# Mixture-of-experts stage of a two-layer kernel: the weight blocks become the stationary operand and the token rows the moving one

## The chip, the cores and the metric

The kernel runs on 1 core of one Trainium2 chip. The metric is the device time of one launch in microseconds. Three runs of the kernel before gave 438.8, 442.28 and 443.53 us; their median is 442.28 us. Matrix products run on TensorE (PE in the profile), with a sequencer of its own that reads its instructions in order (PEldq in the rows); VectorE is DVE, ScalarE is ACT, GpSimd is POOL, SyncE is SP.

## The reference

The input is x, 4 batches of 256 tokens of 128 values. Two layers of cross attention follow, each with a feed-forward part; the last of these is a mixture of 8 experts. All parts add to x. What the change touches is the last one:

```python
t = x.reshape(-1, D)                      # 1024 tokens, D = 128, normalised
probs = jax.nn.softmax(t @ Wg, axis=-1)   # 8 experts
top_v, top_i = jax.lax.top_k(probs, 2)    # two experts for each token
comb = ...                                # their shares, zero elsewhere
for e in range(E):
    h = jax.nn.silu(t @ W1[e]) * (t @ W3[e])      # 512 inner values
    out = out + comb[:, e:e + 1] * (h @ W2[e])    # back to 128
```

## The kernel before

**Attention and the first feed-forward part** fill the first three quarters of the time. Eight passes (two layers of four batches) compute scores, exponentials and the product with the values, head by head, and the other steps of the neighbouring batches are put between the heads.

**The experts.** The 1024 tokens are handled in two halves of 512. Each token has two experts, so a half has 1024 rows. They are sorted by expert into up to 15 slots of 128 rows (`SLOTS`), every slot with a single expert, so there are 30 slots, k = 0 to 29. Which expert a slot has is known only at run time: `expert_id` holds the numbers, and TensorE's sequencer loads the number of slot k with `value_load` (L798) and computes from it the addresses of that expert's weights (`bass.ds(chosen[k], 1)`). A computed address is an instruction of its own on that sequencer (FUSED_REGOPS in the rows). All weights and token rows are kept as two f16 parts, a high and a low one (index s), and a product of two such numbers is made of three matmuls: high by high, high by low, low by high.

A slot goes through three steps:

- `gu` (gate and up, `gate_up`, L811): the 128 token rows, transposed in `takenT`, are the stationary operand and 512 columns of W1[e], then W3[e], move. Three matmuls each, six in all, into `p_misc` and `p_sc`, 128 rows by 512. ACT makes the silu of the first (`gated`, L1327) and DVE multiplies by the second (`product`, L1151) into `hp`.
- `hT` (`hidden_t`, L822): four transposes of 128 by 128 on TensorE turn the product into `p_o`; ACT takes its high part as f16 (`high`, L1333) and DVE the low one (`low`, L1155), into one of two buffers of `hh`.
- `dn` (`down`): four matmuls with both parts of W2[e] side by side as 256 moving columns (L830) and four with the high part alone (L833). ACT copies the columns of the low part to `y_low` (L1339) and DVE adds them (`result`, L1164). The rows of the first half go out by SP (L1580), those of the second by an indirect DMA of POOL (L1438).

**The order of the work** is written down before anything is built: `schedule()` sorts all steps by places from the tables PLACES, SHIFTED and REST, and every engine issues its part of each step in that one order. In the expert stage, `gu` of slot k stands at k, `hT` at k + 1.3 and `dn` at k + 2.6. The first slots share the order with the last pass's projections (L531, L746, L754), the norm of the last tokens, and `compare`, `rank`, `count` and `place`, which sort the second half into its slots. After the last slot, `back` reads the rows from memory and `mix` adds them to x.

Of the kernel before, what the change touches and what calls it, by code (L numbers as in the profile page):

```python
# [5 lines left out]
ALU = mybir.AluOpType  # L6
# [34 lines left out]
    0: {"max": (-4.62, 1.13), "sum": 1.39, "av": (2.76, 1.36), "f_ln": 7.78, "f_xn": -8.15, "f_xT": -1.23,  # L41
        "up0": (-2.85, 0.45), "round": 7.95, "floor": 6.62, "nodes": -8.25, "slope": 5.04, "interp": 7.44,
# [3 lines left out]
        "q0": (6.87, 0.66), "v1": 0.08, "zeros": -2.67, "wipe": -0.41, "init": (2.09, 2.98), "stack": 7.76,  # L46
        "rows": 7.86},
    1: {"max": (9.13, 1.48), "av": (-1.31, 0.11), "f_ln": 12.82, "f_xn": 17.1, "f_xT": -17.07, "up0": (6.69, 1.39),
        "round": -18.46, "floor": 7.56, "nodes": -9.32, "slope": 5.47, "interp": -10.23, "ident": 10.47,
# [3 lines left out]
        "split": (6.74, 1.32), "consts": 0.86, "ex_ln": (0.38, 1.49), "ex_xn": (5.71, 1.53), "ex_xT": (9.95, 0.83),  # L53
        "logits": (1.71, 2.04), "route": 12.72, "shares": 9.48, "compare": 22.49, "rank": 18.69, "best": 28.46,
        "count": 24.36, "place": 10.34, "send": 30.88, "fetch": 3.74, "gT": (17.26, 1.85), "rows": 11.84,
        "weights": 11.47},
# [4 lines left out]
    (0, 'aT'): (4.38, 0.28), (0, 'av'): (-0.45, 0.6), (0, 'bounce'): -1.01, (0, 'down0'): -3.31,  # L61
    (0, 'f_ln'): -7.47, (0, 'f_xT'): -3.24, (0, 'f_xn'): 3.18, (0, 'floor'): 4.93, (0, 'ident'): 3.17,
# [15 lines left out]
    (2, 'interp'): 3.09, (2, 'k0'): (5.7, 0.21), (2, 'k1'): 2.14, (2, 'max'): (1.54, 1.0), (2, 'nodes'): 2.15,
    (2, 'oT'): (5.18, 1.02), (2, 'q0'): (3.7, 1.01), (2, 'q0_ln'): -5.43, (2, 'q0_xT'): -3.12, (2, 'q0_xn'): -1.13,
    (2, 'q1'): 6.18, (2, 'q1_ln'): 4.41, (2, 'q1_xT'): 5.37, (2, 'q1_xn'): 4.83, (2, 'round'): 1.89,  # L80
    (2, 'rows'): 0.74, (2, 'sT'): 3.27, (2, 'slope'): 2.61, (2, 'stack'): -3.62, (2, 'sum'): 2.0,
    (2, 'up0'): (1.55, 0.28), (2, 'v0'): (3.05, 1.03), (2, 'v1'): -0.89, (2, 'wipe'): 5.04,
# [13 lines left out]
    (4, 'max'): (2.36, 1.01), (4, 'nodes'): 4.81, (4, 'oT'): (3.9, 2.04), (4, 'oT1'): (24.7, 0.49),
    (4, 'place'): 10.66, (4, 'q1'): 13.68, (4, 'q1_ln'): 8.29, (4, 'q1_xT'): 11.57, (4, 'q1_xn'): 10.37,
    (4, 'rank'): 17.2, (4, 'round'): 3.81, (4, 'route'): 3.68, (4, 'rows'): 4.05, (4, 'sT'): 3.63,
    (4, 'send'): 20.25, (4, 'shares'): 17.27, (4, 'slope'): 6.05, (4, 'split'): (2.95, 1.2), (4, 'stack'): -0.22,
    (4, 'stage'): (0.67, 1.64), (4, 'up0'): (3.08, 0.42), (4, 'v1'): 5.5, (4, 'weights'): 21.41,  # L100
# [5 lines left out]
    (5, 'logits'): (4.57, 1.56), (5, 'max'): (2.22, 1.14), (5, 'nodes'): 4.91, (5, 'oT'): (-0.41, 1.49),
    (5, 'oT1'): (3.4, 1.43), (5, 'place'): 20.85, (5, 'q1'): 12.67, (5, 'q1_ln'): 6.8, (5, 'q1_xT'): 11.2,
    (5, 'q1_xn'): 9.96, (5, 'rank'): 10.48, (5, 'round'): 2.45, (5, 'route'): 12.73, (5, 'rows'): 1.38,
    (5, 'sT'): -5.5, (5, 'send'): 10.6, (5, 'shares'): 4.61, (5, 'slope'): 4.93, (5, 'split'): (0.78, 2.24),
# [32 lines left out]
def schedule():  # L142
# [127 lines left out]
    for k in range(2 * SLOTS):  # L270
        placed += [(k, ("gu", k)), (k + 1.3, ("hT", k)), (k + 2.6, ("dn", k))]
# [34 lines left out]
def build(nc, t, out):  # L306
    ctx = ExitStack()
    with ctx:
# [215 lines left out]
        def _(pe):  # L524
# [290 lines left out]
            def hidden_t(k):  # L815
                pe.wait_ge(hp_done, k + 1)
                if k == 0:
                    pe.wait_ge(o_free, 6 * B)
                if k >= 2:
                    pe.wait_ge(hl_done, k - 1)  # L820
# [830 lines left out]
```

## Time and profile before

| what | value |
|---|---|
| median of 3 runs | 442.28 us (438.8 to 443.53) |
| the profiled execution's own time | 441.79 us |
| its span | 440.0 us |
| mean granted TensorE clock | 0.944 of full |
| PE / PEld / DVE busy | 87% / 51% / 74% of the span |
| ACT / POOL busy | 55% / 46% of the span |
| last chain: PE / DVE / POOL | 56% / 20% / 7% of the span |

The span runs from the first to the last instruction; 1.8 us lie around it. Busy times of PE contain the time in which a matmul drains while the next one already runs, so the distance between two starts says what one costs and not its duration. Instructions of a sequencer (register work, waits) are not counted as busy. Engine names with a q behind them are sequencers.

### The profile page before, as it was taken

The page shows a single profiled execution, that of the slowest core. Times are in us where ns is not written, and L with a number is a line of the kernel's source. Part 1 is how long each engine was busy: PE and PEld are TensorE (multiplying, and loading weights), DVE is VectorE, ACT ScalarE, POOL GpSimd, SP SyncE. Part 2 cuts the span into 40 slices and gives each one's busy share as a digit, 9 for nine tenths or more (in the row PEclk, how much of TensorE's full clock was granted, in tenths as well). Part 3 has the DMA queues.
Part 4 walks back from the last instruction along what each step waited for, and adds up shares of the span by engine and source line. Part 5 has one row for each costly group of instructions (what it writes and reads, how often), then busy time and mean ns, then how long its engine had stood idle before and what let it go on. Part 6 is the DMA issues. An engine that isn't in the chain of part 4 may idle for free.

```text
span 440.0 us, 8296 instructions
## 1 busy us (share of the span) xinstructions
PE 381.7 (87%) x2779; PEld 223.3 (51%) x2779; DVE 326.9 (74%) x677; ACT 241.4 (55%) x473; POOL 201.3 (46%) x259
## 2 busy tenths in 40 slices
PE   7657799999779968997799889998799889999990
PEld 3414454575356625654544454454355465677660
DVE  5765775667776788888789899889974477676765
ACT  3713455655826471547457858766478644566551
POOL 5034898717363775357052307647141004206661
PEclk9965999999989988998899999999899999999996
DMA  7572717207301802523014203622013001411113
GB/s 188 123 193 52 161 31 165 51 1 176 77 1 37 218 0 62 131 76 117 25 55 119 79 1 109 143 73 73 6 34 103 1 13 43 123 50 49 49 49 97
DMA packets 43406, 34.70 MB, mean 79 GB/s; under 512 B 5901, under 2 KB 39757, under 8 KB 43069
## 3 DMA queue, kind: packets, MB, share of 16 engines
q1 hardware_dynamic: 42117, 31.60, 28.1%
q0 software_dynamic: 1248, 2.57, 1.8%
q8 instruction: 24, 0.39, 0.4%
q14 instruction: 17, 0.14, 0.1%
HBM read 15.13 MB, written 7.89 MB: 52 GB/s over the span
## 4 chain that ended last, share of the span: by engine, by line
PE 56%; DVE 20%; POOL 7%; issue 5%; ACT 5%; SPq 4%; DMA 3%; POOLq 0%; DVEq 0%; ACTq 0%
PE p_sc L630 8%; PE p_o L662 6%; PE p_misc L600 6%; PE p_misc L531 5%; DVE mx L909 5%; PE p_o L649 4%; SPq L1500 4%; PE p_misc L811 4%; PE p_sc L811 4%; PE p_misc L830 3%; PE p_o L822 3%; PE p_misc L704 2%; DVE xn L879 2%; DMA region<-qx 2%; POOL kS L1369 2%
## 5 line engine op out<-in xcount | busy, mean ns | idle before, releaser
L1249 ACT ACTIVATE probs<-p_sc 128x512 f32<-128x512 f32 x192 | 104.6, 597 | 73.8 <-PE p_sc L630 73.1
L909 DVE TENSOR_REDUCE mx<-p_misc 128x1 f32<-128x512 f32 x192 | 121.9, 683 | 16.2 <-PE p_misc L600 15.0
L1363 POOL TENSOR_SCALAR veps<-meanvar 128x2 f32<-128x2 f32 x16 | 3.7, 230 | 101.0 <-DVE meanvar L865 100.7
L600 PE MATMUL p_misc<-kS,qS 96*128 96x512 f16 x128 | 39.9, 387 | 5.4 <-DVE mx L909 5.3
L1405 POOL TENSOR_TENSOR psums<-probs 128x256 f32<-128x256 f32 x32 | 24.4, 763 | 39.7 <-PE p_o L656 35.8
L662 PE MATMUL p_o<-probs,v 128*32 128x256 f32 x512 | 41.6, 402 | 0.6 <-ACT probs L1249 0.6
L630 PE MATMUL p_sc<-qS,kS 128*128 128x256 f16 x256 | 41.2, 281 | 0.3
L649 PE MATMUL p_o<-probs,v 128*64 128x256 f32 x256 | 35.6, 400 | 3.4 <-ACT probs L1249 3.4
L1151 DVE TENSOR_TENSOR probs<-probs,p_sc 128x512 f32<-128x512 f32 x30 | 20.6, 685 | 22.8 <-ACT probs L1327 22.5
L630 PE MATMUL p_sc<-region 128*128 128x256 f16 x256 | 35.4, 284 | 2.2 <-DVE region L923 2.2
L1327 ACT ACTIVATE probs<-p_misc 128x512 f32<-128x512 f32 x30 | 17.9, 597 | 31.5 <-PE p_sc L811 31.5
L630 PEld LDWEIGHTS p_sc<-qS,kS 128*128 128x128 f16 x256 | 21.7, 99 | 21.4 <-issue 12.3
L630 PEld LDWEIGHTS p_sc<-region 128*128 128x128 f16 x256 | 24.7, 102 | 14.0 <-issue 5.1
L1460 POOL TENSOR_TENSOR region<-v,region 128x512 f16<-128x512 f32 x24 | 28.8, 1200 | 1.9
L1406 POOL TENSOR_TENSOR psums<-psums,probs 128x256 f32<-128x256 f32 x32 | 27.1, 845 | 2.5
L600 PE MATMUL p_misc<-region 128*128 128x512 f16 x64 | 21.1, 404 | 6.9 <-DVE cT L893 3.0
L1407 POOL TENSOR_TENSOR psums<-psums,probs 128x256 f32<-128x256 f32 x32 | 24.8, 774 | 2.5
L649 PEld LDWEIGHTS p_o<-probs,v 128*64 128x64 f32 x256 | 15.9, 138 | 18.4 <-issue 10.0
L1459 POOL CAST region<-v 128x512 f16<-128x512 f32 x24 | 15.4, 640 | 14.3 <-DMA v<-in_L_ffn_W_dram 13.4
L1155 DVE TENSOR_TENSOR probs<-p_o,probs 128x512 f16<-128x512 f32 x30 | 20.5, 684 | 1.6 <-ACT probs L1333 1.6
L879 DVE TENSOR_SCALAR xn<-x_sb,meanvar,rstd 128x128 f32<-128x128 f32 x24 | 15.0, 705 | 8.5 <-issue 5.0
L600 PEld LDWEIGHTS p_misc<-kS,qS 96*128 96x128 f16 x128 | 11.6, 100 | 17.5 <-DVE mx L909 9.4
(221 smaller groups left out, 763.7 us busy)
## 6 DMA issues: line engine op xcount, KB each, us to landing
region<-kx SPq DMA_DIRECT2D x24, 256.0 KB, 3.9
v<-in_L_ffn_W_dram SPq DMA_DIRECT2D x24, 256.0 KB, 2.7
region<-qx SPq DMA_DIRECT2D x24, 128.0 KB, 3.8
kS<-kS SPq DMA_DIRECT2D x1, 1664.0 KB
kS<-k_scratch SPq DMA_DIRECT2D x8, 192.0 KB
k_scratch<-kx SPq DMA_DIRECT2D x4, 256.0 KB, 2.8
slots_in<-qS SPq DMA_DIRECT2D x1, 975.0 KB, 10.0
slots_in<-qS SPq DMA_DIRECT2D x1, 960.0 KB, 6.0
```

The lines of the kernel that those rows point to most:

```text
L600: pe.matmul(ps, q[:, i * P:(i + 1) * P], k, start=True, stop=True).then_inc(full, 1)
L630: last = pe.matmul(p_sc[:, half, j * S:(j + 1) * S], k[:, kt * P:(kt + 1) * P], q, start=(i == 0), stop=(i == len(pairs) - 1))
L649: pe.matmul(p_o[64 * i:64 * i + 64, 0, m * S:(m + 1) * S], v0[:, b % 2, kt, h * DH0:(h + 1) * DH0], probs[:, h % 8, kt * S:(kt + 1) * S], ...
L662: last = pe.matmul(p_o[32 * j:32 * j + 32, n % 2, 0:S], v1[:, b % 2, c, h * VW:h * VW + 32], probs[:, h % 8, c * S:(c + 1) * S], start=(c ...
L811: last = pe.matmul(ps[:, k % 2, :], takenT[half][:, xs, at], w[:, bass.ds(chosen[k], 1), ws, :].rearrange("p e n -> p (e n)"), start=(i == ...
L879: last = dve.tensor_scalar(dst, x_sb[:, b * T + i, :], meanvar[:, n % 2, i, 0:1], rstd[:, n % 2, i:i + 1], ALU.subtract, ALU.mult)
L909: dve.tensor_reduce(mx[:, b % 2, i, h:h + 1], ps, AX_X, ALU.max).then_inc(free, 1)
L1249: act.activation(probs[:, h % 8, half * 512:(half + 1) * 512], p_sc[:, half, :], ACT.Exp, scale=(DH0 if layer == 0 else DH1) ** -0.5).then ...
L1405: link(pool.tensor_tensor(psums[:, h % 4, :], tiles[0], tiles[1], ALU.add))
L1406: link(pool.tensor_tensor(psums[:, h % 4, :], psums[:, h % 4, :], tiles[2], ALU.add))
L1407: pool.tensor_tensor(psums[:, h % 4, :], psums[:, h % 4, :], tiles[3], ALU.add).then_inc(sums_set, 1)
L1460: pool.tensor_tensor(low, whole, high, ALU.subtract).then_inc(stage_free, 1)
```

## The change

Slots, experts, the three-matmul products and the results stay as they are. In `gate_up` a block of 128 weight columns is now the stationary operand and the 128 token rows move, so that the output comes out with the inner values on the partitions. The transposes (`hidden_t`) go. DVE writes the product straight into `p_o`, from which ACT and DVE take the high and low parts as before, into four buffers of `hh` instead of two. `down` is written as three passes over four blocks with 128 moving columns each, all into the same 128 columns; `y_low` and DVE's addition go, and ACT's copy (`result`) writes `y_sb` itself. `dn` stands at k + 3.1 instead of k + 2.6. The numbers in PLACES, SHIFTED and REST are new throughout; the set of steps that they place is the same.

```diff
@@ schedule()
-        placed += [(k, ("gu", k)), (k + 1.3, ("hT", k)), (k + 2.6, ("dn", k))]
+        placed += [(k, ("gu", k)), (k + 1.3, ("hT", k)), (k + 3.1, ("dn", k))]
...
-    placed += [(SLOTS + 4.9 + 3.8 * i, ("mix", 0, i)) for i in range(NT)]
+    placed += [(SLOTS + 4.7 + 3.8 * i, ("mix", 0, i)) for i in range(NT)]
@@ buffers
-        hp = probs[:, 1, :].rearrange("p (a b) -> p a b", a=2)
-        hh = probs[:, 2, :].bitcast(F16).rearrange("p (b s n) -> p b s n", b=2, s=2)
-        y_low = probs[:, 3, 0:2 * P].rearrange("p (b n) -> p b n", b=2)
+        hh = probs[:, 1:3, :].rearrange("p i n -> p (i n)").bitcast(F16).rearrange("p (b s n) -> p b s n", b=4, s=2)
@@ TensorE, gate_up
-                    for i, (ws, xs) in enumerate(((0, 0), (0, 1), (1, 0))):
-                        last = pe.matmul(ps[:, k % 2, :], takenT[half][:, xs, at], w[:, bass.ds(chosen[k], 1), ws, :].rearrange("p e n -> p (e n)"),
-                                         start=(i == 0), stop=(i == 2))
+                    for f in range(FF):
+                        block = slice(f * P, (f + 1) * P)
+                        for i, (ws, xs) in enumerate(((0, 0), (0, 1), (1, 0))):
+                            last = pe.matmul(ps[:, k % 2, block], w[:, bass.ds(chosen[k], 1), ws, block].rearrange("p e n -> p (e n)"),
+                                             takenT[half][:, xs, at], start=(i == 0), stop=(i == 2))
...
-            def hidden_t(k):
...
-                for f in range(FF):
-                    last = pe.transpose(p_o[:, k % 2, f * P:(f + 1) * P], hp[:, k % 2, f * P:(f + 1) * P], ident[:, :])
-                last.then_inc(hT_full, 1)
@@ TensorE, down
-                for f in range(FF):
-                    w = ew2[:, bass.ds(chosen[k], 1), f, :, :].rearrange("p e s n -> p (e s n)")
-                    pe.matmul(ps[:, 0:2 * P], hh[:, k % 2, 0, f * P:(f + 1) * P], w, start=(f == 0), stop=False)
-                for f in range(FF):
-                    w = ew2[:, bass.ds(chosen[k], 1), f, 0, :].rearrange("p e n -> p (e n)")
-                    last = pe.matmul(ps[:, 0:P], hh[:, k % 2, 1, f * P:(f + 1) * P], w, start=False, stop=(f == FF - 1))
+                for hs, ws in ((0, 0), (0, 1), (1, 0)):
+                    for f in range(FF):
+                        w = ew2[:, bass.ds(chosen[k], 1), f, ws, :].rearrange("p e n -> p (e n)")
+                        last = pe.matmul(ps[:, 0:P], hh[:, k % 4, hs, f * P:(f + 1) * P], w,
+                                         start=(hs == ws == f == 0), stop=(hs == 1 and f == FF - 1))
@@ VectorE, product and low; result is gone
+                if k == 0:
+                    dve.wait_ge(o_free, 6 * B)
                 if k >= 2:
-                    dve.wait_ge(hT_full, k - 1)
-                dve.tensor_tensor(hp[:, k % 2, :], sg[:, k % 2, :], p_sc[:, k % 2, :], ALU.mult).then_inc(hp_done, 1)
+                    dve.wait_ge(hl_done, k - 1)
+                dve.tensor_tensor(p_o[:, k % 2, :], sg[:, k % 2, :], p_sc[:, k % 2, :], ALU.mult).then_inc(hp_done, 1)
...
@@ ScalarE, high and result
-                act.wait_ge(hT_full, k + 1)
-                if k >= 2:
-                    misc_wait(act, ("ym", k - 2))
-                act.copy(hh[:, k % 2, 0, :], p_o[:, k % 2, :]).then_inc(hh_done, 1)
+                act.wait_ge(hp_done, k + 1)
+                if k >= 4:
+                    misc_wait(act, ("ym", k - 4))
+                act.copy(hh[:, k % 4, 0, :], p_o[:, k % 2, :]).then_inc(hh_done, 1)
...
-                act.copy(y_low[:, k % 2, :], ps[:, P:2 * P]).then_inc(y_half, 1)
+                if 4 <= k < SLOTS + 4:
+                    act.wait_ge(y_kept[k % 4], 16 * (k // 4))
+                elif k >= 4:
+                    act.wait_ge(y_sent[k % 4], 16 * sent_of(k - 4))
+                ps, free = misc_wait(act, ("ym", k))
+                act.copy(y_sb[:, k % 4, :], ps[:, 0:P]).then_inc(free, 1)
```

## Rows read from the trace of the kernel before

**Rows 1.** Busy time by stretch of the span; columns as in the second line.
```profile
core 0: us, PE busy (x) PEld busy (x) DVE busy (x) ACT busy (x) POOL busy (x), PEclk, DMA share, GB/s
0.00:344.35 344.35, 301.22 (x2188) 168.27 (x2188) 263.00 (x508) 194.11 (x371) 170.13 (x226) 0.94 0.34 86
344.35:369.52 25.17, 20.86 (x146) 13.35 (x143) 17.27 (x57) 11.69 (x24) 3.04 (x5) 1.00 0.05 14
369.52:429.94 60.42, 59.58 (x449) 41.68 (x449) 41.07 (x89) 33.82 (x76) 26.62 (x28) 1.00 0.22 64
```

**Rows 2.** Timeline of TensorE in one slot: start us, us, engine, line, tiles, count.
```profile
402.17 0.82 PE L811 MATMUL p_misc<-region,probs 128*128 x3
402.83 0.81 PE L811 MATMUL p_sc<-region,probs 128*128 x3
403.48 0.60 PE L822 MATMUL p_o<-ident,probs 128*128 128x128 f32 x4
403.91 0.60 PE L830 MATMUL p_misc<-region,probs 128*128 x4
404.35 0.39 PE L833 MATMUL p_misc<-region,probs 128*128 x4
```

**Rows 3.** Instructions of lines L811, L830, L833 in the whole span, duration ns min/median/max.
```profile
L811 PEldq FUSED_REGOPS  x120: 46/46/51, 344.1 to 424.2; - x120
...
L830 PEldq FUSED_REGOPS  x120: 46/46/46, 353.9 to 429.3; - x120
...
L833 PEld LDWEIGHTS p_misc<-region,probs x120: 97/98/99, 355.6 to 429.7; 128*128 128x128 f16 x120
L833 PE MATMUL p_misc<-region,probs x120: 219/219/219, 355.7 to 429.7; 128*128 x120
```

**Rows 4.** One stretch of TensorE's sequencer, line by line, 384.98 to 386.88 us.
```profile
L830 PEldq FUSED_REGOPS  x4: 46/46/46, 385.0 to 385.4; - x4
...
L495 PEldq EVENT_SEMAPHORE  x1: 51/51/51, 385.5 to 385.5; - x1
...
L798 PEldq TENSOR_LOAD <-kx x1: 313/313/313, 385.7 to 385.7; - x1
...
L811 PEldq FUSED_REGOPS  x4: 46/46/51, 386.3 to 386.7; - x4
...
L820 PEldq EVENT_SEMAPHORE  x1: 51/51/51, 386.8 to 386.8; - x1
```

**Rows 5.** Timeline of TensorE and its weight loads in the last slot.
```profile
429.06 0.65 PE L830 MATMUL p_misc<-region,probs 128*128 x4 [0.49 <-DVE probs L1155]
429.55 0.39 PE L833 MATMUL p_misc<-region,probs 128*128 x4
...
429.05 0.47 PEld L830 LDWEIGHTS p_misc<-region,probs 128*128 128x128 f16 x4 [0.66 <-issue]
```

**Rows 6.** Timeline of TensorE: twelve 128-column matmuls at the full clock and at half.
```profile
287.96 0.84 PE L722 MATMUL p_misc<-wc,cT 96*128 96x128 f16 x12
...
206.57 1.46 PE L722 MATMUL p_misc<-wc,cT 96*128 96x128 f16 x12 [2.35 <-DVE mx L909]
```

**Rows 7.** ACT and DVE groups, 369.5 to 427.6 us: count | busy us, mean ns | idle before, releaser.
```profile
L1155 DVE TENSOR_TENSOR probs<-p_o,probs 128x512 f16<-128x512 f32 x24 | 16.4, 683 | 0.0
L1151 DVE TENSOR_TENSOR probs<-probs,p_sc 128x512 f32<-128x512 f32 x23 | 15.8, 687 | 18.4 <-ACT probs L1327 18.4
...
L1327 ACT ACTIVATE probs<-p_misc 128x512 f32<-128x512 f32 x23 | 13.7, 597 | 23.5 <-PE p_sc L811 23.5
L1333 ACT CAST probs<-p_o 128x512 f16<-128x512 f32 x23 | 13.3, 580 | 0.0
...
L1164 DVE TENSOR_TENSOR probs<-p_misc,probs 128x128 f32<-128x128 f32 x24 | 6.7, 281 | 0.0
```

**Rows 8.** Stretches on either side of a fall of the granted clock.
```profile
247.50:250.90 3.40, 1.67 (x14) 0.46 (x12) 3.30 (x5) 3.25 (x5) 0.00 (x0) 0.99 0.23 86
250.90:254.30 3.40, 3.25 (x18) 1.66 (x18) 3.33 (x8) 3.34 (x5) 0.00 (x0) 0.51 0.00 0
```

More of the change, by code:

```diff
@@ L40 @@
 PLACES = {
-    0: {"max": (-4.62, 1.13), "sum": 1.39, "av": (2.76, 1.36), "f_ln": 7.78, "f_xn": -8.15, "f_xT": -1.23,
-        "up0": (-2.85, 0.45), "round": 7.95, "floor": 6.62, "nodes": -8.25, "slope": 5.04, "interp": 7.44,
[3 rows of a table removed]
[L46 to L49, printed above, removed]
[3 rows of a table removed]
[L53 to L56, printed above, removed]
+    0: {"max": (-8.6, 1.13), "sum": 3.84, "av": (2.9, 1.22), "f_ln": 8.5, "f_xn": -7.99, "f_xT": -4.13,
+        "up0": (-3.54, 0.17), "round": 5.08, "floor": 6.91, "nodes": -8.63, "slope": 4.85, "interp": 6.1,
[3 rows of a table added]
+        "v1": -1.81, "zeros": -3.28, "wipe": -0.5, "init": (1.97, 2.97), "stack": 8.35, "rows": 7.72},
@@ new lines @@
+    1: {"max": (11.48, 1.51), "av": (2.56, 0.11), "f_ln": 8.48, "f_xn": 17.13, "f_xT": -14.69, "up0": (9.56, 1.5),
+        "round": -19.3, "floor": 1.49, "nodes": -4.8, "slope": 15.47, "interp": -7.65, "ident": 10.47,
[3 rows of a table added]
+        "split": (6.95, 0.95), "consts": 4.58, "ex_ln": (3.19, 1.49), "ex_xn": (1.82, 1.53),
+        "ex_xT": (10.28, 0.83), "logits": (2.65, 1.87), "route": 14.84, "shares": 10.12, "compare": 21.68,
+        "rank": 19.76, "best": 30.35, "count": 24.36, "place": 5.14, "send": 31.74, "fetch": 3.15,
+        "gT": (18.67, 2.21), "rows": 11.04, "weights": 10.64},
@@ L78 @@
[L78 to L82, printed above, removed]
@@ L96 @@
[L96 to L100, printed above, removed]
@@ L106 @@
[L106 to L109, printed above, removed]
-    (5, 'stack'): -8.2, (5, 'stage'): (-1.47, 2.13), (5, 'up0'): (2.12, 0.29), (5, 'v1'): 6.14,
@@ L116 @@
-    (6, 'k1'): 5.74, (6, 'logits'): (10.56, 1.25), (6, 'max'): (3.51, 1.26), (6, 'nodes'): -12.77,
-    (6, 'oT'): (9.36, 2.42), (6, 'oT1'): (5.29, 0.4), (6, 'place'): 15.05, (6, 'q1'): -4.01, (6, 'q1_ln'): 8.43,
-    (6, 'q1_xT'): 8.06, (6, 'q1_xn'): 13.98, (6, 'rank'): 13.35, (6, 'round'): -7.01, (6, 'route'): 11.83,
-    (6, 'rows'): 2.88, (6, 'sT'): -6.41, (6, 'send'): 21.24, (6, 'shares'): 13.9, (6, 'slope'): 2.81,
-    (6, 'split'): (0.76, 1.9), (6, 'stack'): -25.07, (6, 'stage'): (1.91, 2.25), (6, 'up0'): (-3.67, 0.22),
@@ L131 @@
[L131 to L139 removed]
+    (0, 'aT'): (4.27, 0.05), (0, 'av'): (-0.45, 0.6), (0, 'bounce'): 0.43, (0, 'down0'): -4.63, (0, 'f_ln'): -9.28,
@@ new lines @@
+    (2, 'round'): 1.89, (2, 'rows'): 0.7, (2, 'sT'): 3.42, (2, 'slope'): 2.67, (2, 'stack'): -2.07,
+    (2, 'sum'): 2.0, (2, 'up0'): (1.55, 0.14), (2, 'v0'): (3.05, 1.03), (2, 'v1'): -1.53, (2, 'wipe'): 3.84,
+    (2, 'y0'): (6.02, 1.79), (2, 'zeros'): 10.52, (3, 'aT'): (5.57, 1.84), (3, 'av'): (-0.45, 0.96),
+    (3, 'bounce'): 4.5, (3, 'down0'): 4.29, (3, 'f_ln'): -7.72, (3, 'f_xT'): 1.43, (3, 'f_xn'): 0.9,
+    (3, 'floor'): 1.79, (3, 'ident'): 3.84, (3, 'init'): (1.35, 1.95), (3, 'interp'): 3.55,
[3 rows of a table added]
@@ new lines @@
+    (3, 'sT'): 3.85, (3, 'slope'): 3.39, (3, 'stack'): -11.49, (3, 'sum'): 1.18, (3, 'up0'): (1.55, 0.05),
+    (3, 'v0'): (-0.24, 0.41), (3, 'v1'): 4.99, (3, 'wipe'): -0.66, (3, 'y0'): (7.01, 0.68), (3, 'zeros'): 2.49,
+    (4, 'aT'): (5.9, 2.15), (4, 'aT1'): 2.68, (4, 'av'): (-0.1, 1.02), (4, 'best'): 9.03, (4, 'bounce'): 12.73,
+    (4, 'compare'): 15.92, (4, 'consts'): 1.28, (4, 'count'): 5.69, (4, 'down0'): 7.86,
+    (4, 'ex_ln'): (11.92, 2.75), (4, 'ex_xT'): (12.88, 0.95), (4, 'ex_xn'): (0.95, 1.31), (4, 'f_ln'): 1.18,
@@ new lines @@
+    (4, 'send'): 20.04, (4, 'shares'): 17.27, (4, 'slope'): 5.84, (4, 'split'): (2.95, 1.27), (4, 'stack'): -0.22,
+    (4, 'stage'): (0.67, 1.49), (4, 'up0'): (3.08, 0.42), (4, 'v1'): 5.36, (4, 'weights'): 20.92,
+    (4, 'y0'): (6.3, 2.78), (4, 'y1'): -5.14, (5, 'aT'): (-10.57, 1.21), (5, 'aT1'): 5.06, (5, 'av'): (0.27, 1.06),
+    (5, 'best'): 19.51, (5, 'bounce'): 10.27, (5, 'compare'): 10.26, (5, 'consts'): 5.65, (5, 'count'): 12.49,
+    (5, 'down0'): 6.53, (5, 'ex_ln'): (12.17, 0.05), (5, 'ex_xT'): (10.39, 0.07), (5, 'ex_xn'): (5.32, 1.26),
@@ new lines @@
+    (5, 'sT'): -5.61, (5, 'send'): 10.6, (5, 'shares'): 4.61, (5, 'slope'): 4.93, (5, 'split'): (0.78, 2.17),
+    (5, 'stack'): -8.59, (5, 'stage'): (-1.31, 2.29), (5, 'up0'): (2.12, 0.29), (5, 'v1'): 6.14,
+    (5, 'weights'): 12.63, (5, 'y0'): (13.47, 3.01), (5, 'y1'): 16.07, (6, 'aT'): (10.66, 1.64), (6, 'aT1'): 6.96,
+    (6, 'av'): (1.47, 0.73), (6, 'best'): 18.34, (6, 'bounce'): 5.03, (6, 'compare'): 12.04, (6, 'consts'): 2.32,
+    (6, 'count'): 14.95, (6, 'down0'): -3.42, (6, 'ex_ln'): (8.32, 1.06), (6, 'ex_xT'): (10.42, 0.67),
@@ new lines @@
+    (6, 'rows'): 3.01, (6, 'sT'): -4.97, (6, 'send'): 21.28, (6, 'shares'): 16.27, (6, 'slope'): 2.03,
+    (6, 'split'): (0.76, 1.9), (6, 'stack'): -26.53, (6, 'stage'): (2.77, 2.25), (6, 'up0'): (-4.94, 0.08),
+    (6, 'v1'): 3.98, (6, 'weights'): 28.88, (6, 'y0'): (-1.33, 4.04), (6, 'y1'): 8.62, (7, 'aT'): (-17.99, 1.14),
+    (7, 'aT1'): 7.17, (7, 'av'): (0.44, 1.18), (7, 'best'): 29.98, (7, 'bounce'): 29.7, (7, 'compare'): 19.6,
+    (7, 'consts'): 12.25, (7, 'count'): 8.3, (7, 'down0'): 2.78, (7, 'ex_ln'): (10.0, 0.5),
@@ new lines @@
+    (7, 'rank'): 8.8, (7, 'round'): -7.97, (7, 'route'): 7.02, (7, 'rows'): 7.01, (7, 'sT'): -12.46,
+    (7, 'send'): 39.69, (7, 'shares'): 7.02, (7, 'slope'): 14.49, (7, 'split'): (1.23, 2.1), (7, 'stack'): 9.96,
+    (7, 'stage'): (1.82, 1.73), (7, 'up0'): (2.3, 0.64), (7, 'v1'): -4.88, (7, 'weights'): 16.47,
+    (7, 'y0'): (-4.34, 1.77), (7, 'y1'): 9.76}
+REST = [(0.0, 'oT1', 3, 0), (0.0, 'oT1', 3, 1), (1.05, 'aT1', 3), (1.67, 'h1', 3), (1.72, 'y1', 3),
+        (1.75, 'ln', 'ex', 3), (2.42, 'xn', 'ex', 3), (3.31, 'xT', 'ex', 3), (3.57, 'logits', 3),
+        (3.89, 'compare', 1), (3.92, 'rank', 1), (4.78, 'count', 1), (4.87, 'place', 1), (9.96, 'send', 1),
+        (11.23, 'fetch', 1), (14.01, 'gT', 1, 0), (15.21, 'dest'), (17.19, 'gT', 1, 1), (18.57, 'gT', 1, 2),
+        (21.71, 'gT', 1, 3), (26.1, 'route', 1), (39.62, 'shares', 1), (40.73, 'best', 1), (54.8, 'weights', 1)]
```

109 lines of the change are left out of this document (41 added, 68 removed), and 28 rows, old and new, of tables (PLACES, SHIFTED).

## The prediction

> **What bounds the kernel now.** I first cut the span at the expert stage [rows 1]. From 344.35 us, where slot 0's first matmul starts, to 369.52, where slot 7's does, TensorE is busy for 20.86 of 25.17 us: the last projections and the sorting of the second half stand between the slots. From there to its last matmul, at 429.94, it is busy for 59.58 of 60.42 us. Then 10.06 us without TensorE bring the rows back. The attention before 344.35 has none of the changed lines.
>
> Next, what a slot costs TensorE, from distances of starts [rows 2]. Six matmuls of 512 columns: 403.48 - 402.17 = 1.31 us, about 0.216 each. Four transposes: 0.43. Four matmuls of 256 columns: 0.44. Four of 128 columns: three distances in 0.39 - 0.219 [rows 2, 3], so 0.057 each, 0.22. Together 2.40 us. The stretch holds 23 `gu`, 24 `hT`, 25 `dn` and 15 other transposes: 138 x 0.216 + 96 x 0.109 + 100 x 0.109 + 100 x 0.056 + 15 x 0.109 = 58.4 of 60.4 us. So the data path bounds it. ACT and DVE are well below: 0.60 + 0.58 us and a short copy, and 0.69 + 0.68 + 0.28 us a slot [rows 7].
>
> Third, TensorE's sequencer, which busy shares leave out. L811 and L830 each have 120 address instructions, 4 for each of 30 slots [rows 3]. `gu` has four distinct weight addresses (two matrices, two parts), though six matmuls use them; the four of L833 point where L830's did, and that line shows none. So the count is one for each distinct address, and it is kept for a second use. Their recorded 46 ns is not their price. In a stretch without a wait [rows 4] four address instructions, a semaphore wait, the load of the expert's number, four more address instructions and the next wait start between 385.0 and 386.8 us. The load group takes 385.7 to 386.3, about 0.64 us; the nine others share the remaining 1.16, 0.125 to 0.13 us each. Among L830's four lie three matmuls with their loads, among L811's four lie five, and both take the same 0.4 us: to the sequencer the matmuls themselves are nearly free. The last slot shows the same on the engine [rows 5]: when TensorE has nothing queued, L830's four weight loads take 0.47 us, (0.47 - 0.098) / 3 = 0.124 us apart. A slot now asks the sequencer for 8 x 0.125 + 0.64 + 2 waits x 0.125 = 1.9 us, hidden under 2.4 us of matmuls.
>
> **The change, part by part.**
>
> Data path. `gu`: 24 matmuls of 128 columns, each with its own weight load, at 0.056 us = 1.34 us, against 1.31. Twelve such matmuls in a row took 0.84 us at the full clock, (0.84 - 0.22) / 11 = 0.056 [rows 6]. `hT` goes: -0.44. `dn`: 12 x 0.056 = 0.67, against 0.66. A slot takes 2.0 us, 0.4 less. The Trainium skill has a rule against this change (TensorE: Matmul & The Clock Gate, Back-to-back issue gap): pairs of weight load and 128-column matmul sustain only about 81 ns each. By it a slot would take an estimated 36 x 0.081 = 2.9 us. The trace does not agree: 0.056.
>
> Sequencer. `gu` now addresses four blocks of two parts of two matrices: 16 distinct addresses, not 4. `dn` addresses four blocks of two parts: 8, not 4; its third pass uses the first's again. So 24 instead of 8. One `gu` costs 16 x 0.125 + 0.64 = 2.64 us, one `dn` 8 x 0.125 + 0.125 for its wait = 1.125 us. The wait of `hT` goes. A slot costs 3.77 us of sequencer, more than the 2.0 us of matmuls and the 2.4 us of now: **the sequencer becomes the bound**. Bounds per slot: from below 2.0 us, the data path, if an address cost only its recorded 46 ns (24 x 0.046 + 0.64 + 0.125 = 1.87); from above 24 x 0.13 + 0.64 + 0.25 = 4.0. I take 3.77, as both views of the pace agree. That recorded time understates a sequencer's instruction is also in the Trainium skill (Perfetto Trace Analysis, Sequencer-only Instruction): the wait before and the push after are not recorded. By 46 ns the change would gain; by the spacing, which the trace shows, it loses.
>
> From slot 7's start to the last matmul the new order holds 23 `gu` and 26 `dn` (slots 4 to 29): 23 x 2.64 + 26 x 1.125 + 4 waits of the second half's transposes = 60.7 + 29.3 + 0.5 = 90.5 us, against 60.42: **+30.1 us**. The deep order hides the waits: `dn` stands three slots behind its `gu`, over 10 us, and its chain on ACT and DVE is four instructions of 0.58 to 0.69 us.
>
> The first seven slots, 25.17 us: their sequencer work is 7 x 2.64 + 4 x 1.125 = 23 us, but it is split by waits for ACT and DVE, behind which it cannot run ahead. If all added addresses lie bare: 7 x 12 x 0.125 + 4 x 4 x 0.125 = 12.5. If the waits cover them: 0. Up to the second projection there are gaps for it; after it two `gu` and a `dn` stand ahead of the norm's transposes and delay the sorting. I take **+3**, near the covered end, because 23 fits in 25.
>
> Removed on ACT and DVE: DVE's 0.28 us of L1164 per slot, nothing, since neither bounds; on the last slot it is bare, with a handoff: **-0.4**. ACT's copy takes over its waits for `y_sb`; behind it in ACT's queue stands the next slot's `silu`, but the store that it waits for was issued four slots earlier, 15 us, so nothing. DVE writing PSUM instead of SBUF: 0.69 us is taken as before; L1155, which reads PSUM, has 0.68. It has room to double. `high` waits for slot k - 4 instead of k - 2: nothing.
>
> The new tables. Sorting the steps by the old and the new tables, 335 of 747 change their position, most by one to five; the largest moves are the bounce of batch 1 (28 earlier) and of batch 0 (7 later) on SP's queue, POOL's weight splits (up to 5), `shares` and `route`. Their cover is the idle time of TensorE before 344.35 (43 us) and nothing says which way it goes: 0, with 3 us either way, within the 4.7 us that the runs differ by.
>
> Sum: 440.0 + 30.1 + 3 - 0.4 = 472.7 us of span, 474.5 with the 1.8 us around it. The profiled execution's own time is 0.5 below the median, so about 474 to 475.
>
> **The rivals.**
>
> *The sequencer does not bind (faster).* If two parts 128 or 512 columns apart shared a register, or an address came at its 46 ns, the data path would decide: 864 matmuls x 0.056 + 1.6 = 50.0 us against 58.4, -8.4, another -1 in the first slots, -0.4 at the end: 432 us. It decides once a slot's sequencer work is under 2.0 us. Against it: two parts did not share one [rows 3], and the live spacing [rows 5]. Left open: the moving operand had the computed address, now the stationary one has it. 0.11.
>
> *The clock falls too.* One of the falls of the granted clock to half (1.2 GHz) came after a stretch with TensorE busy for 1.67 of 3.40 us [rows 8]. Here its matmuls fill 2.0 of 3.77 us. At half clock twelve take 1.46 us [rows 6], 0.105 to 0.12 each: 36 x 0.11 = 4.0 us a slot, a little over the sequencer, and gaps no longer overlap well: 4.1 to 4.3, 23 to 25 slots, +8 to +13: 484 us. Against it: the row's busy share also counts draining, and by that count TensorE would stay near 80% busy. 0.12.
>
> *Weight loads stop overlapping*, while addresses are cheap. A load takes 98 ns [rows 3] and now has 0.056 us of columns above it; if loads ran one after another, 864 x 0.098 + 1.6 = 86.3 against 58.4, +28: 470 us, with sequencer gaps of no account. Rows 6 speak against it: twelve loads and matmuls in 0.84 us. 0.04. This is what the rule of the Trainium skill named above comes to; with its 81 ns the same sum would be 455 us, an estimate.
>
> *No change*, by a partial sharing of addresses at which sequencer and gain cancel (2.4 us a slot): 442. 0.03.
>
> **How the numbers follow.** The forecast has 0.70. Its own range is 464 (nothing in the first slots, tables -3, 3.6 us a slot) to 484 (12.5 in the first slots); the clock case reaches 489. The range 463 to 489 leaves out the first and the fourth rival and the forecast's far ends. A change of about 1% is what this kernel's runs can tell: faster 0.12, same 0.03, slower 0.85 (0.70, 0.12 and 0.04, rounded down).
>
> **What would show it.** Lines of `gu` with 480 address instructions and of `dn` with 240; their spacing 0.125 us; weight loads of TensorE idle before them by "issue"; slots 3.7 to 3.8 us apart; no change in the duration of the matmuls, ACT and DVE. It is wrong if slots come 2.0 to 2.4 us apart, or if the address count stayed near 240.

## The result, and the profile after

The changed kernel takes 476.69 us (median of 4 runs, 475.46 to 478.15); the kernel before took 441.8 (4 runs). The ratio is 1.080, with a 95% interval of 1.073 to 1.087: slower by 35 us, where the forecast had 474. The profiled execution took 477.52 us, its span is 475.7.

The first view is again the span cut at slot 0, slot 7 and the last matmul; it answers to [rows 1] (the same columns: us, busy time and count of PE, PEld, DVE, ACT, POOL, PEclk, DMA share, GB/s).

```profile
0.00:340.60 340.60, 301.00 (x2189) 167.48 (x2189) 262.71 (x508) 193.94 (x371) 169.65 (x226) 0.94 0.35 87
340.60:370.70 30.10, 25.98 (x256) 20.77 (x252) 16.22 (x52) 10.82 (x23) 3.98 (x6) 0.89 0.04 12
370.70:465.82 95.12, 86.40 (x879) 64.46 (x879) 38.89 (x66) 34.66 (x77) 25.59 (x27) 1.00 0.14 42
465.82:475.70 9.88, 0.04 (x1) 0.00 (x0) 4.87 (x21) 1.78 (x3) 1.44 (x2) 0.57 0.32 98
```

The stretch from slot 7 on grew from 60.42 to 95.12 us. PE is still busy for 91% of it, which looks like a full engine. That is the trap of this case: a matmul is recorded with 0.219 us, of which 0.056 is its share of the pace when the queue is full and some 0.16 is draining, so matmuls that start 0.06 to 0.12 us apart record as one unbroken stretch. 864 matmuls at 0.056 us and 15 transposes at 0.109 are 50 us of work, about half of the 95.

The next rows, of lines L810 (gate and up) and L820 (down) in the whole span, answer to [rows 3].

```profile
L810 PEldq FUSED_REGOPS  x480: 46/46/51, 340.4 to 459.9; - x160
...
L820 PE MATMUL p_misc<-region,probs x360: 219/227/228, 355.8 to 465.6; 128*128 x180
L820 PEldq FUSED_REGOPS  x240: 46/46/46, 355.6 to 465.3; - x120
```

There are 480 and 240 computed addresses, 16 and 8 a slot. One slot of the sequencer, 434.5 to 438.4 us, answers to [rows 4]:

```profile
L810 PEldq FUSED_REGOPS  x16: 46/46/46, 434.6 to 436.6; - x16
...
L492 PEldq EVENT_SEMAPHORE  x1: 51/51/51, 436.7 to 436.7; - x1
...
L820 PEldq FUSED_REGOPS  x8: 46/46/46, 436.8 to 437.7; - x8
...
L795 PEldq TENSOR_LOAD <-kx x1: 303/303/303, 437.8 to 437.8; - x1
L795 PEldq FUSED_REGOPS  x1: 151/151/151, 438.2 to 438.2; - x1
```

In this slot the sequencer never rests: addresses, the wait, addresses, the load of the next number, each record 0.12 us or a little more after the one before. And this is what TensorE does in that slot, the timeline that answers to [rows 2]:

```profile
434.71 1.13 PE L810 MATMUL p_misc<-probs,region 128*128 128x128 f16 x12 [0.32 <-DVE p_o L1141]
...
435.74 1.19 PE L810 MATMUL p_sc<-probs,region 128*128 128x128 f16 x12
...
436.93 1.34 PE L820 MATMUL p_misc<-region,probs 128*128 x12
...
438.59 1.12 PE L810 MATMUL p_misc<-probs,region 128*128 128x128 f16 x12 [0.32 <-DVE p_o L1141]
```

Slot 23 to slot 24 is 438.59 - 434.71 = 3.88 us, where [rows 2] had 2.40 without the second half's transposes. Twelve matmuls take 1.13 us here and took 0.84 with the queue full [rows 6]. The releaser in brackets, DVE's product, is a wrong name: that product ended at 434.39, and this step waits for the one two slots back (`hp_done` in `gate_up`). The summary of waits (engine, line, what it waited for: us in total, times, longest) says it better for the weight loads:

```profile
PEld p_misc L810 <- issue: 13.8, 29, 1.5
PEld p_misc L820 <- issue: 1.9, 7, 0.8
```

"Issue" is idle time in which the engine waited for nothing that the profile shows, that is for its own sequencer. It comes 29 times ahead of the first weight load of a slot, where the sequencer loads the expert's number.

### The profile page after: what moved, and what is told of

It is laid out like the page before. It is cut to its first block, busy times and chain, and to the rows that moved or that the text cites. A ratio compares the mean times of both kernels' runs of the same rounds, so it can differ in the third digit from the quotient of the medians.

```text
span 475.7 us, 9765 instructions
## 1 busy us (share of the span) xinstructions
PE 413.4 (87%) x3319; PEld 252.7 (53%) x3319; DVE 322.7 (68%) x647; ACT 241.2 (51%) x473; POOL 200.7 (42%) x259
## 4 chain that ended last, share of the span: by engine, by line
PE 59%; DVE 16%; ACT 8%; issue 6%; SPq 4%; DMA 3%; POOL 2%; POOLq 0%; ACTq 0%; DVEq 0%
PE p_sc L627 9%; PE p_misc L810 7%; PE p_sc L810 6%; PE p_misc L597 6%; PE p_o L659 5%; PE p_o L646 5%; PE p_misc L528 5%; DVE mx L897 4%; SPq L1483 4%; PE p_misc L820 3%; DVE p_o L1141 3%; ACT probs L1308 2%; PE p_misc L554 2%; PE p_misc L701 2%; DMA region<-qx 2%
## 5 line engine op out<-in xcount | busy, mean ns | idle before, releaser
L1141 DVE TENSOR_TENSOR p_o<-probs,p_sc 128x512 f32<-128x512 f32 x30 | 20.9, 695 | 42.8 <-ACT probs L1308 41.3
L597 PE MATMUL p_misc<-kS,qS 96*128 96x512 f16 x128 | 41.1, 394 | 5.4 <-DVE mx L897 3.8
L1388 POOL TENSOR_TENSOR psums<-probs 128x256 f32<-128x256 f32 x32 | 25.1, 783 | 39.5 <-PE p_o L653 36.6
L820 PE MATMUL p_misc<-region,probs 128*128 x360 | 39.9, 224 | 1.0 <-DVE probs L1145 0.6
L820 PEld LDWEIGHTS p_misc<-region,probs 128*128 128x128 f16 x360 | 28.4, 96 | 11.3 <-issue 1.9
L1389 POOL TENSOR_TENSOR psums<-psums,probs 128x256 f32<-128x256 f32 x32 | 26.4, 826 | 2.5
L1390 POOL TENSOR_TENSOR psums<-psums,probs 128x256 f32<-128x256 f32 x32 | 24.4, 763 | 2.5
L1421 POOL DMA_INDIRECT token_rows<-probs,kx x15 | 14.5, 967 | 25.9 <-ACT probs L1322 25.0
```

The source lines that it names most:

```text
L597: pe.matmul(ps, q[:, i * P:(i + 1) * P], k, start=True, stop=True).then_inc(full, 1)
L820: last = pe.matmul(ps[:, 0:P], hh[:, k % 4, hs, f * P:(f + 1) * P], w, start=(hs == ws == f == 0), stop=(hs == 1 and f == FF - 1))
L1141: dve.tensor_tensor(p_o[:, k % 2, :], sg[:, k % 2, :], p_sc[:, k % 2, :], ALU.mult).then_inc(hp_done, 1)
L1389: link(pool.tensor_tensor(psums[:, h % 4, :], psums[:, h % 4, :], tiles[2], ALU.add))
```

## The experiments

Every ratio is to runs of the kernel before on the same chip. Their medians were 440.86 us (fixed experts, one load, high part only, four blocks), 440.07 (two blocks, down step of before, old tables, new tables) and 439.91 (no bounds check, mixed tables, every third slot). The distance between slots is the median from slot 7 to slot 29, read in the timeline.

**Fixed experts.** No weight address is computed.

```diff
... in gate_up
-  w[:, bass.ds(chosen[k], 1), ws, block].rearrange("p e n -> p (e n)")
+  w[:, k % E, ws, block]
... in down
-  ew2[:, bass.ds(chosen[k], 1), f, ws, :].rearrange("p e n -> p (e n)")
+  ew2[:, k % E, f, ws, :]
```

> The changed kernel, with the expert of slot k fixed in the program (k mod 8), so that no weight address is computed; the loads of the experts' numbers stay. It leaves out the choice of the experts. Theory (the sequencer's computed addresses, 24 a slot at 0.124 us, set the expert stage): no address instructions, slots at the data path's 36 x 0.056 = 2.0 us instead of 3.9; from slot 7 on 50 us instead of 95, the first seven slots back from 30 to about 25: 427 us (423 to 433). Rival (many small pairs of weight load and matmul cost this by themselves): 470 to 477 us.

It took 432.77 us (ratio to before 0.980, 0.973 to 0.987), 44 us less than the change, with the same 36 pairs of weight load and matmul a slot. Slots are 2.01 us apart, the data path's sum. The timeline of TensorE shows full pace, and where most of the missing 5.8 us to the 427 expected went:

```profile
377.80 0.83 PE L820 MATMUL p_misc<-region,probs 128*128 128x128 f16 x12
378.47 0.83 PE L810 MATMUL p_misc<-kS,region 128*128 128x128 f16 x12
379.14 0.83 PE L810 MATMUL p_sc<-kS,region 128*128 128x128 f16 x12
381.67 0.66 PE L528 MATMUL p_misc<-ident,kS 128*128 128x128 f32 x4 [1.69 <-DMA kS<-slots_in]
382.16 0.83 PE L820 MATMUL p_misc<-region,probs 128*128 128x128 f16 x12
384.46 1.46 PE L810 MATMUL p_misc<-probs,region 128*128 128x128 f16 x12 [1.47 <-DVE probs L1115]
```

Slot 14 to slot 15 took 384.46 - 378.47 = 5.99 us: TensorE reached the second half before its rows had landed, and slot 15 began at the half clock (1.46 us for twelve). The chain that brings the second half's rows is the next wait. So even without addresses this kernel gains 8 us on the kernel before and not 14. The gain isn't all the turned form's: of the 7.9 us that this trace's span is shorter, 5.05 lie ahead of slot 0 (339.30 against 344.35 us), where nothing is turned and only the order is new; from slot 7 to the last matmul it took 56.17 us against 60.42, 4.25 less.

**One load for each half.** The addresses still come from registers, but they are computed once and stay.

```diff
+  chosen[k] = pe.value_load(...) if j == 0 else chosen[k - 1]
```

> The changed kernel, with one load of the expert's number for each half, used for all its 15 slots, so that the 24 addresses are computed once a half and stay in registers; weight loads and matmuls still take their addresses from registers. It leaves out the choice of the experts for all but the first slot of a half. Theory (only computing an address costs, using it is free): slots at 2.0 us, 427 us (423 to 433), as with fixed experts. Rival (a stationary operand with its address in a register is slow in itself; only the loads of 0.64 us a slot go): 477 - 28 x 0.64 = 459 us.

435.3 us (0.985, 0.979 to 0.992), above the 423 to 433 expected, but far from the rival's 459; slots 2.01 us apart. Rows of L810 and L820:

```profile
L810 PEldq FUSED_REGOPS  x32: 46/46/46, 340.1 to 388.3; - x32
...
L820 PEldq FUSED_REGOPS  x16: 46/46/46, 354.7 to 396.5; - x16
```

48 computations instead of 720. Between slots of one half, a stationary operand with its address in a register costs nothing over a fixed one; computing the address does. Against the trace with fixed experts, slot 0 began 1.0 us later, 1.0 us went into the first seven slots (26.1 against 25.1 us), where 24 addresses are computed, and 0.9 us into the stretch from slot 7 to slot 29, which has the 24 of the second half. The largest part of what lies over the 427 us is, as with fixed experts, the wait ahead of slot 15, which came 6.0 us after slot 14.

**Half of the gate and up addresses.** All three matmuls of a block read the high part.

```diff
-  w[:, bass.ds(chosen[k], 1), ws, block]...
+  w[:, bass.ds(chosen[k], 1), 0, block]...
```

> The changed kernel, with the high part of the gate and up weights used in all three matmuls of a block: 8 addresses in gate_up instead of 16, all 36 matmuls stay. It leaves out the low part of these weights. Theory: 16 addresses a slot, 3.9 - 8 x 0.124 = 2.9 us; 23 slots and the first ones give back 25 to 30 us: 449 us (446 to 453). Rival (price by matmuls, not addresses): 477 us.

450.41 us (1.023, 1.018 to 1.029). L810 has 240 address instructions; two slots of the timeline start 2.92 us apart, the median is 2.90:

```profile
402.97 0.84 PE L810 MATMUL p_misc<-probs,region 128*128 128x128 f16 x12
...
405.89 0.84 PE L810 MATMUL p_misc<-probs,region 128*128 128x128 f16 x12 [0.32 <-DVE p_o L1141]
```

Eight addresses fewer, with the same 36 matmuls, give 3.91 - 2.90 = 1.01 us a slot back, 0.126 each.

**The kernel before with its gate and up cut into four column blocks.** Tokens stay stationary, the transposes stay, the order stays.

```diff
-                    for i, (ws, xs) in enumerate(((0, 0), (0, 1), (1, 0))):
-                        last = pe.matmul(ps[:, k % 2, :], takenT[half][:, xs, at], w[:, bass.ds(chosen[k], 1), ws, :]...
+                    for f in range(4):
+                        block = slice(f * 128, (f + 1) * 128)
+                        for i, (ws, xs) in enumerate(((0, 0), (0, 1), (1, 0))):
+                            last = pe.matmul(ps[:, k % 2, block], takenT[half][:, xs, at], w[:, bass.ds(chosen[k], 1), ws, block]...
```

> The kernel before, with the gate and up matmuls cut into four column blocks each (24 matmuls of 128 moving columns instead of 6 of 512; tokens stay stationary, transposes and all else stay): 20 addresses a slot instead of 8, the same columns. Theory: sequencer 20 x 0.124 + 0.64 + 0.25 = 3.4 us, with the 0.15 us on top that the slots of the changed kernel showed 3.5; against 2.46 before that is +26 us from slot 7 on and about +3 ahead of it: 471 us (464 to 475). Rival (the turned operands or the new order cost the time): 442 us, same as before.

467.82 us (1.063, 1.056 to 1.070): the loss without the change. Its timeline has the transposes and the full columns of before, and still loses:

```profile
424.96 1.12 PE L813 MATMUL p_misc<-region,probs 128*128 x12
425.97 1.13 PE L813 MATMUL p_sc<-region,probs 128*128 x12
427.00 0.63 PE L824 MATMUL p_o<-ident,probs 128*128 128x128 f32 x4
427.46 0.60 PE L832 MATMUL p_misc<-region,probs 128*128 x4
427.90 0.39 PE L835 MATMUL p_misc<-region,probs 128*128 x4
428.50 1.14 PE L813 MATMUL p_misc<-region,probs 128*128 x12 [0.21 <-DVE probs L1153]
```

A slot takes 428.50 - 424.96 = 3.54 us. Neither the turn nor the new order is needed for the loss. Many matmuls and weight loads alone don't make it either: with fixed experts the change has more of them and no loss.

**The same with two blocks.**

```diff
+                    for f in range(2):
+                        block = slice(f * 256, (f + 1) * 256)
...
```

> The kernel before with the gate and up matmuls cut into two column blocks each (12 matmuls of 256 columns): 12 addresses a slot instead of 8. Theory: sequencer 12 x 0.124 + 0.64 + 0.25, and the 0.15 us that slots with 16, 20 and 24 addresses had on top, 2.53 us, just over the 2.39 us of matmuls: +3 us, 444 us (441 to 446). Rival (each address adds its 0.124 us from the first on): 30 x 4 x 0.124 = 15 us more, 457 us. Rival (a price by matmuls with loads, not addresses): 30 x 6 more pairs, nothing.

441.85 us (1.005, 1.002 to 1.009), 1.8 us above the median of the kernel before. Slots are 2.50 us apart at the median. It excludes that every address adds its price from the first on: four more a slot would be 15 us. The addresses begin to cost where the sequencer's time passes the data path's.

**The change with the down step of before.** The wide moving operand, `y_low` and DVE's addition come back.

```diff
-                for hs, ws in ((0, 0), (0, 1), (1, 0)):
-                    for f in range(FF):
-                        w = ew2[:, bass.ds(chosen[k], 1), f, ws, :]...
+                for f in range(FF):
+                    w = ew2[:, bass.ds(chosen[k], 1), f, :, :]...
+                    pe.matmul(ps[:, 0:2 * P], hh[:, k % 4, 0, f * P:(f + 1) * P], w, start=(f == 0), stop=False)
+                for f in range(FF):
+                    w = ew2[:, bass.ds(chosen[k], 1), f, 0, :]...
```

> The changed kernel with the down step of the kernel before: both parts of W2 side by side as 256 moving columns, y_low and the addition on VectorE back; 4 addresses in it instead of 8, 8 matmuls instead of 12 with the same columns. Theory: 20 addresses a slot, 3.9 - 0.5 = 3.4 us: 477 - 26 x 0.5 + 0.4 = 464 us (461 to 467). Rival (the price is in gate_up's form alone): 477 us.

463.77 us (1.053, 1.046 to 1.059). Slots 3.42 us apart: four addresses fewer give 0.49 us back, 0.12 each, this time in `down`. This kernel also has four matmuls fewer a slot, of the same columns in all; the kernel with the high part alone, which keeps all 36, says that it is the addresses.

**No bounds check.** The load stays, its 151 ns of register work and the assertion go.

```diff
-  chosen[k] = pe.value_load(expert_id[0:1, half, j:j + 1], min_val=0, max_val=E - 1)
+  chosen[k] = nc.values_load(expert_id[0:1, half, j:j + 1], engines=[mybir.EngineType.PE], min_val=0, max_val=E - 1,
+                             skip_runtime_bounds_check_because=...)
```

> The changed kernel, with the expert's number loaded without its bounds check: the load group's 151 ns of register work and its assertion go (place() has bounded the number already), the load and all 24 addresses stay. Theory (everything on TensorE's sequencer counts there once it is the bound): 0.209 + 0.077 = 0.29 us less a slot; 25 to 30 slots: 477 - 8 = 469 us (467 to 471). Rival (only computed addresses count, the load group overlaps with them): 477 us.

468.48 us (1.064, 1.060 to 1.069), slots 3.62 us apart, 0.29 less than 3.91, as reckoned. The load group is a plain term of the sum.

**Old tables in the change.**

```diff
-PLACES, SHIFTED, REST = ...   # as changed
+PLACES, SHIFTED, REST = ...   # as before
```

> The changed kernel with the tables PLACES, SHIFTED and REST of the kernel before (the places of the slots' own steps, k + 1.3 and k + 3.1, stay as changed). In the changed kernel's trace slot 0 began at 340.6 us, in the trace before at 344.35. Theory A (the new tables shortened the attention by 3.8 us): 477 + 4 = 481 us, slot 0 at about 344. Rival B (the 3.8 us are one execution's chance): 477 us. Either way slots stay 3.9 us apart.

478.9 us, a ratio of 1.085 (1.080 to 1.090) where the change had 1.080 (1.073 to 1.087): the intervals overlap, and the difference of some 2 us is not settled by them. In its trace slot 0 began at 343.41 us instead of 340.60, and the stretch from slot 7 on took 94.19 instead of 95.12. Whether slot 0's start is one execution's chance is answered by all the traces together: in the five kernels with the old PLACES and SHIFTED it began at 341.75 to 344.60 us, in the eight with the new ones at 338.37 to 340.60. The two groups don't overlap, and their means are 3.95 us apart, so the new tables do shorten the attention, whatever the experts do behind it.

**New tables in the kernel before**, and then **the new PLACES and SHIFTED with the old REST**.

```diff
-PLACES, SHIFTED, REST = ...   # as before
+PLACES, SHIFTED = ...         # as changed, in both
+REST = ...                    # as changed in the first, as before in the second
```

> The kernel before with the new tables PLACES, SHIFTED and REST (slots' own steps as before, k + 1.3 and k + 2.6): all of the order's change without the change of the experts. Theory A (the tables are worth 3.8 us ahead of slot 0): 438 us, faster than both kernels. Rival B: 442 us. Slots 2.4 us apart in both.

> The kernel before with the new PLACES and SHIFTED and its own REST, the order of the steps among the slots. With all three new tables slot 0 came 5.8 us earlier in the trace, but the first seven slots took 0.8 and the rest 2.6 us more. Theory A (the longer slots come from the new REST): slot 0 stays early and the slots get back to 25.2 and 60.4 us: 437 us. Rival B (starting slots earlier only moves them into the wait for the second half's rows, whose chain is long in itself): 440 us, the same as before.

With all new tables 440.09 us (0.999, 0.996 to 1.002): no change, so theory A's 438 did not come. With the mixed ones 436.91 us (0.993, 0.990 to 0.995) against 437 expected: 0.7% less than the kernel before, and the fastest of the kernels here that leave nothing out. The windows by stretch, with the columns of [rows 1], first of the kernel with all new tables, then of the mixed one:

```profile
0.00:338.53 338.53, 298.05 (x2189) 166.54 (x2189) 262.72 (x508) 193.94 (x371) 169.37 (x226) 0.95 0.35 87
338.53:364.46 25.93, 20.71 (x147) 13.39 (x143) 17.26 (x57) 11.72 (x24) 3.02 (x5) 1.00 0.04 13
364.46:427.44 62.98, 60.22 (x449) 41.62 (x449) 41.10 (x91) 33.54 (x76) 26.57 (x28) 1.00 0.21 61
```

```profile
0.00:339.38 339.38, 297.98 (x2189) 165.72 (x2189) 262.40 (x508) 193.97 (x371) 169.63 (x226) 0.94 0.35 87
339.38:364.55 25.17, 20.81 (x146) 13.38 (x143) 17.27 (x57) 11.71 (x24) 3.02 (x5) 1.00 0.05 13
364.55:425.10 60.55, 59.62 (x449) 41.65 (x449) 40.92 (x89) 33.77 (x76) 26.70 (x28) 1.00 0.22 64
```

The new PLACES and SHIFTED bring slot 0 forward by 5 to 6 us against [rows 1]; the new REST gives 3.2 us of it back among the slots, 0.8 and 2.4 us more than with the old one. In the first of the two kernels TensorE waits ahead of slot 15 for the low part of the second half's rows:

```profile
385.67 0.82 PE L810 MATMUL p_misc<-region,probs 128*128 x3 [1.40 <-DVE probs L1126]
```

With the old REST that wait is not in the trace. The device times show less than the slot 0 of these two traces does: 3 us, not 5.

**Every third slot turned.** The kernel before without the bounds check, with 7 of its 30 slots turned.

```diff
+        def turned(k):
+            return k >= 8 and k % 3 == 1
...
+                    if turned(k):
+                        for f in range(FF):      # 24 matmuls, weights stationary
...
+                (p_o if turned(k) else hp)[:, k % 2, :]
```

> The kernel before, bounds check off, with every third slot from 10 on (7 slots) turned as in the change: its product goes straight to p_o and has no transposes; the down step stays as before. A turned slot asks 20 addresses, about 3.1 us of sequencer and 2.0 us of matmuls; the two between ask 1.6 and 2.39. Theory (what bounds is the sum over the slots that the queue ahead of TensorE can even out): three slots need 6.3 us of sequencer and 6.8 of matmuls: 7 x 0.39 = 2.7 us gained, 438 us. Rival (the queue evens out too little, and TensorE runs dry in each turned slot): 3.1 - 2.39 = 0.7 us lost seven times, 445 us.

443.48 us (1.007, 1.004 to 1.010): the theory that three slots are evened out fell, the rival came near. (The kernel before without the bounds check alone was not run; the ratio is to the kernel with it.) The timeline of slot 16 of that kernel:

```profile
392.74 0.83 PE L823 MATMUL p_misc<-probs,region 128*128 128x128 f16 x12
393.41 1.13 PE L823 MATMUL p_sc<-probs,region 128*128 128x128 f16 x12
394.44 0.63 PE L840 MATMUL p_o<-ident,probs 128*128 128x128 f32 x4
```

Here the first twelve run at full pace on what was queued (0.83), the second twelve at the sequencer's (1.13). Slot 16 is the best of the seven: it has four extra transposes ahead of it, and in the other six the first twelve took 0.91 to 1.25 us. Slot 25 shows why. The rows are the sequencer's last wait for a free bank (L495), its addresses of `down` (L848), those of the turned slot (L823), and TensorE:

```profile
L495 PEldq EVENT_SEMAPHORE  x1: 51/51/51, 414.5 to 414.5; - x1
...
L848 PEldq FUSED_REGOPS  x4: 46/46/46, 415.1 to 415.5; - x4
...
L823 PEldq FUSED_REGOPS  x16: 46/46/46, 415.9 to 417.9; - x16
...
416.04 1.14 PE L823 MATMUL p_misc<-probs,region 128*128 128x128 f16 x12
417.07 1.13 PE L823 MATMUL p_sc<-probs,region 128*128 128x128 f16 x12
```

The first address of the turned slot is computed 0.1 us before TensorE starts it: nothing lies queued. In the slots between, where it has time to spare, the sequencer does not run ahead but stands in its waits. That of `down` for the low part of `hh` (L848, ended by DVE at 415.04) takes 0.58 us here instead of 0.11, that for a free bank up to 1.05 us more than its 0.12. In the changed kernel neither wait is in the way: the sequencer is late there. So this run shows that the slack of the other slots cannot be saved up past these waits; how much a full queue could cover it does not show. A part of the loss is another wait, the transposes' for DVE's product, 1.4 us in two places from slot 7 on.

## Why the prediction was right

**The count.** 16 + 8 addresses a slot were forecast, 480 and 240 stand in the trace. The rule, one for each distinct address, kept for a second use, gives the count of every kernel here, down to 48 for the whole kernel with one load a half.

**The price.** 0.125 us from the spacing and not the recorded 46 ns was right: 0.126 in gate and up, 0.12 in down, by the kernels that took them away.

**The bound.** The distances of slots line up by the addresses that are computed, whatever the operands' roles:

| kernel | addresses computed a slot | slot, us |
|---|---|---|
| fixed experts, turned | 0 | 2.01 |
| one load for each half, turned | 0, but for two slots | 2.01 |
| before | 8 | 2.39 |
| before, two blocks | 12 | 2.50 |
| turned, high part only | 16 | 2.90 |
| turned, wide down | 20 | 3.42 |
| before, four blocks | 20 | 3.55 |
| turned, no bounds check | 24 | 3.62 |
| turned (the change) | 24 | 3.91 |

The two kernels with 20 differ by 0.13, one more instruction's time: the wait of the transposes that one still has. Where the matmuls cease to hide the sequencer can be estimated from the table: 3.55 - 20 x 0.125 = 1.05 us are left without addresses, and (2.39 - 1.05) / 0.125 is about 11 for the kernel before; for the turned form, with 3.91 - 24 x 0.125 = 0.91 and 2.01 us of matmuls, it is about 9. No run lies between 0 and 16 addresses there.

That 46 ns are recorded where 124 pass agrees with what the Trainium skill says of instructions that only a sequencer executes (Perfetto Trace Analysis, Sequencer-only Instruction): part of their time is not in the profile. What the other 78 ns are, no run here shows.

**The size.** Four terms, against what the trace measured:

| term | forecast | measured |
|---|---|---|
| slot 7 to the last matmul | +30.1 | 95.12 - 60.42 = +34.7 |
| the first seven slots | +3 | 30.10 - 25.17 = +4.9 |
| attention, new tables | 0 (within 3) | 340.60 - 344.35 = -3.75 |
| after the last matmul | -0.4 | 9.88 - 10.06 = -0.2 |
| sum | +32.7 | +35.7 |

The first was 4.6 us short. A slot was taken as 3.77 us and is 3.91: over 22 distances 3.1 us. The 24 addresses, the wait and the load are 3.75 us at their even pace; the rest, 0.15 us a slot, is single spacings that are longer (16 addresses take 434.6 to 436.6, where 15 x 0.124 is 1.86), whose cause no run here shows. And slot 15 came 5.05 us after slot 14, 1.1 us more, since it waits for the low part of the second half's rows; with the old tables that wait is absent (94.19 us). The second term was near its covered end, as argued, but 2 us short. The addresses are the cause here too: this stretch took 25.10 us with fixed experts, 26.99 with 16 addresses a slot and 29.00 with four blocks in the kernel before. In it the clock did fall once, behind a stretch with TensorE busy for 1.99 of 3.40 us, and the projections ran at half (PEclk in the second and third row; columns as above):

```profile
344.00:347.40 3.40, 1.99 (x21) 1.41 (x19) 2.21 (x6) 1.74 (x5) 0.00 (x0) 1.00 0.00 0
347.40:350.80 3.40, 2.47 (x8) 1.68 (x9) 0.69 (x1) 1.19 (x3) 0.00 (x0) 0.56 0.00 0
350.80:354.20 3.40, 3.40 (x30) 3.34 (x29) 1.59 (x6) 0.00 (x0) 0.30 (x2) 0.50 0.02 5
```

The fall alone does not make the 4.9 us: PEclk over the whole stretch is 0.89 here, 0.86 with fixed experts, which took no longer than before, and 1.00 with four blocks, which lost 3.8 us all the same. What the fall adds no run separates.

The tables' term was put at 0 for want of a reason, with 3 us either way; the -3.75 lies outside that, and the traces of the other kernels show it as an effect of the tables. It paid for more than half of the 6.7 us that the others lacked. That the forecast's 474 is so near to 476.7 is luck in part.

**The rivals.** The clock stayed at full from slot 7 on (PEclk 1.00), while the rows count PE busy for 86.40 of 95.12 us, as the argument against that rival had it. Weight loads do overlap: with fixed experts 36 of them with their matmuls take 2.01 us, 0.056 each. The 81 ns of the Trainium skill (TensorE: Matmul & The Clock Gate, Back-to-back issue gap) do not hold in this kernel: it is 56 in 17 of the 22 distances behind slot 7, seven of them in a row. The rival that ended faster failed on both of its conditions: two parts do not share a register (16 addresses a slot in `gu`), and an address comes at 0.124 us and not at 0.046. The rival without a change needed 2.4 us a slot and would have shown fewer than 24 addresses.

## What to carry to other kernels

Count the distinct run-time addresses of an engine's instructions and price them by the spacing of a sequencer's records, not by their duration; do it beside the sum of the data path, since the larger of the two is the time. Turning the operands so that a transpose goes away costs weight blocks, and where these are picked at run time each block is one more address: compute it once for many uses, or keep the picked operand the wide moving one. A busy share of 91% hid that this engine had half of its time to spare; the distance between starts showed it.

## What was not expected of the hardware

Slots that ask about 3.1 us of the sequencer, between slots that ask about 1.6 and have some 0.8 us to spare, were not evened out (every third slot turned, 443.48 us where 438 was reckoned). In that trace TensorE's sequencer, which reads in order, stood in waits for other engines ahead of every turned slot, in a single one for up to 1.05 us over its pace, and computed the slot's first address only 0.10 to 0.46 us before TensorE started the slot. Time that a sequencer has to spare is lost at such a wait.

Pairs of a weight load and a 128-column matmul held 0.056 us each over whole slots, although a load is recorded with 0.098 us: with fixed experts 36 pairs took 2.01 us.
